# Softmax on the 16 scores a row owns, not on all 128, in the merged attention stage of a two-layer gated transformer

## The reference

```
Q = (layernorm(x) @ Wq.T + bq).reshape(bs, sl, 16, 32)
K = (ctx @ Wk.T + bk).reshape(bs, sl, 16, 32)
V = (ctx @ Wv.T + bv).reshape(bs, sl, 16, 32)
score  = einsum('bshd,bsgd->bshg', Q, K)
weight = softmax(score, axis=-1)            # over the 16 heads g of the same token
attn   = einsum('bshg,bsgd->bshd', weight, V).reshape(bs, sl, 512)
x = x + tanh(g_xattn[1]) * (attn @ Wo.T + bo)
```

## Time and profile before

| | us |
|---|---|
| median of 3 runs | 2135.85 (2131.82 to 2138.77) |
| profiled execution | 2135.37, its span 2133.6 |
| PE busy | 1943.9 (91%) |
| POOL busy | 1085.6 (51%) |
| DVE busy | 993.3 (47%) |
| ACT busy | 832.2 (39%) |
| mean granted TensorE clock | 0.952 of 2.4 GHz |

### The profile page before, as it was taken

The page is one execution under the profiler, slowest core; times in us unless marked ns, Lnnn a source line. Parts: engine busy times, 40 slices in busy tenths (PEclk is TensorE's granted clock), DMA queues, the critical chain, the costliest instruction groups (busy, mean ns, idle before and its releaser), DMA issues. The chain is left out here.

```text
span 2133.6 us, 29710 instructions
## 1 busy us (share of the span) xinstructions
PE 1943.9 (91%) x10300; PEld 1621.4 (76%) x10300; DVE 993.3 (47%) x1565; ACT 832.2 (39%) x1588; POOL 1085.6 (51%) x815
## 2 busy tenths in 40 slices
PE   6999999999999999969999899996499976899998
PEld 5888788878888789847777799995377754678886
DVE  3547654765475556553341233335366343673111
ACT  3327333633354333531112122223277766443332
POOL 5765476548754774442138737514344322844332
PEclk9999999999999999979999899998699977899999
DMA  4231333033322322352327655325678454431000
GB/s 148 95 109 51 114 104 128 30 108 110 109 70 74 124 99 80 120 184 84 126 82 239 215 160 171 115 65 172 171 193 215 125 139 158 159 99 49 20 20 20
DMA packets 172237, 248.12 MB, mean 116 GB/s; under 512 B 44944, under 2 KB 69520, under 8 KB 172112
## 3 DMA queue, kind: packets, MB, share of 16 engines
q1 hardware_dynamic: 157024, 202.09, 30.0%
q0 software_dynamic: 9472, 34.09, 5.0%
q10 hardware_dynamic: 5616, 10.23, 1.2%
HBM read 179.77 MB, written 66.58 MB: 115 GB/s over the span
## 5 line engine op out<-in xcount | busy, mean ns | idle before, releaser
L255 POOL TENSOR_TENSOR a_w_hl<-a_w_raw,a_w_hl 128x2048 fp32r<-128x2048 f32 x63 | 290.7, 4614 | 151.5 <-ACT a_w_hl L320 151.5
L436 PE MATMUL a_proj<-a_c_hl,a_w_hl 128*128 128x512 f32 x768 | 185.1, 401 | 21.0 <-DVE a_w_hl L556 19.8
L436 PEld LDWEIGHTS a_proj<-a_c_hl,a_w_hl 128*128 128x128 f32 x768 | 147.8, 194 | 53.1 <-issue 19.8
L510 PE MATMUL a_proj<-a_w_hl,a_a_hl 128*128 128x512 f32 x768 | 179.5, 392 | 3.9 <-DVE a_a_hl L612 3.9
L320 ACT ACTIVATE a_w_hl<-a_w_raw 128x2048 fp32r<-128x2048 f32 x64 | 122.4, 1912 | 151.7 <-PE a_proj L436 106.7
L436 PE MATMUL a_proj<-a_w_hl,a_c_hl 128*128 128x512 f32 x768 | 181.3, 392 | 0.0
L339 ACT ACTIVATE a_sq<-a_proj,a_vecs 128x512 f32<-128x512 f32 x128 | 88.0, 690 | 232.7 <-PE a_proj L436 160.4
L436 PE MATMUL a_proj<-a_a_hl,a_w_hl 128*128 128x512 f32 x768 | 176.4, 390 | 0.0
L510 PEld LDWEIGHTS a_proj<-a_w_hl,a_a_hl 128*128 128x128 f32 x768 | 142.7, 188 | 34.3 <-POOL a_w_hl L255 5.5
L436 PEld LDWEIGHTS a_proj<-a_a_hl,a_w_hl 128*128 128x128 f32 x768 | 143.6, 188 | 29.7
L279 POOL TENSOR_TENSOR a_ssum<-a_ssum,a_sq 128x512 f32<-128x512 f32 x112 | 145.3, 1297 | 40.1 <-ACT a_sq L339 35.5
(11 more groups left out here) (251 smaller groups left out, 3628.2 us busy)
## 6 DMA issues: line engine op xcount, KB each, us to landing
a_w_raw<-in_a_ki_w SPq DMA_DIRECT2D x16, 1024.0 KB, 5.1
a_w_raw<-in_a_vi_w SPq DMA_DIRECT2D x16, 1024.0 KB, 4.9
a_w_raw<-in_a_q_w SPq DMA_DIRECT2D x16, 1024.0 KB, 4.9
a_w_raw<-in_a_o_w SPq DMA_DIRECT2D x16, 1024.0 KB, 5.3
spare<-in_b_gate_up POOLq DMA_DIRECT2D x32, 352.0 KB, 3.8
l_sorted_rows<-b_zeros SPq DMA_DIRECT2D x39, 256.0 KB, 3.2
spare<-l_sorted_rows SPq DMA_DIRECT2D x39, 256.0 KB, 3.2
l_expert_out<-spare ACTq DMA_DIRECT2D x39, 256.0 KB, 3.5
```

What stands on the lines that cost most here:

```text
L255: pool.tensor_tensor(w_hl[:, s, 1], w_raw[:, s], f32(w_hl[:, s, 0]), ALU.subtract)\
L436: mm = pe.matmul(proj[:, j, :], left, right, start=(k == 0 and n == 0), stop=(k == KC - 1 and n == 2))
L510: mm = pe.matmul(proj[:, j, :], a_hl[:, ap, k, j * P:(j + 1) * P], w_hl[:, i % 2, wp, k], start=(n == 0 and m == 0), stop=(n == 4 * G - 1 ...
```

## The change

In the loop, DVE now multiplies a unit's scores by a 0/1 mask and sums over the 8 tokens of a tile, which leaves each row's own 16 scores (`own_scores`). The maximum, the subtraction, the sum, the reciprocal and the product then run on DVE for a whole pair at once, on 128 x 128 elements (`subtract_max`, `normalise`); ACT takes one exponent per pair, and POOL spreads the result over the 128-wide tile behind the mask (`expand`). `turn` now stands two pairs behind, `weigh` three. The order of items changes too: the prologue holds k, v, h, q of block 0 and k of block 1, the loop then h and v alternately, q, and the next block's k. `move_queries` moves to w = 7, `load_q` to w = 6, the tiles' statistics to w = 4 to 7, the splitting of the context to w = 4 and 5. The low parts of Wq and of context block 1 move from POOL to DVE in the prologue. At each barrier POOL clears the semaphores of the stage before the one that ends, and does so ahead of the barrier.

```diff
-    BIG = 1e30
     RING = 6
-    LAG = 2
+    TURN_LAG, LAG = 2, 3
     IN_QK = NQ * 16
 
-    ITEMS = [(kind, b, j) for kind, b in (("k", 0), ("v", 0), ("h", 0), ("q", 0), ("h", 1), ("q", 1)) for j in range(4)]
+    def four(kind, b):
+        return [(kind, b, j) for j in range(4)]
+
+    ITEMS = four("k", 0) + four("v", 0) + four("h", 0) + four("q", 0) + four("k", 1)
     FIRST = len(ITEMS)
     for n in range(1, NBLK):
-        ITEMS += [("k", n, j) for j in range(4)]
+        ITEMS += [(kind, n, j) for j in range(4) for kind in "hv"] + four("q", n)
         if n + 1 < NBLK:
-            ITEMS += [("v", n, 0), ("h", n + 1, 0), ("v", n, 1), ("h", n + 1, 1), ("h", n + 1, 2), ("h", n + 1, 3),
-                      ("v", n, 2), ("v", n, 3)]
-            ITEMS += [("q", n + 1, j) for j in range(4)]
-        else:
-            ITEMS += [("v", n, j) for j in range(4)]
+            ITEMS += four("k", n + 1)
     NI = len(ITEMS)
     AT = {item: i for i, item in enumerate(ITEMS)}
-    ROUND = {kb: n for n, kb in enumerate((k, b) for k, b, j in ITEMS if k != "h" and j == 0)}
+    ROUND = {item: sum(k != "h" and j == item[2] for k, b, j in ITEMS[:i]) for i, item in enumerate(ITEMS)}
...
+        masked_sc = sb("masked_sc", [P, UN, P])
+        own_sc = sb("own_sc", [P, 3, 2, UN, H])
+        mx = sb("mx", [P, 2, 2 * UN])
+        den = sb("den", [P, 2, 2 * UN])
+        rden = sb("rden", [P, 2, 2 * UN])
...
-        for p in range(12, NP * NBLK):
-            PIECES += [(p, "act")] + ([(p, "dve")] if p >= 20 else [])
+        for p in range(2 * NP, NP * NBLK):
+            PIECES += [(p, "act"), (p, "dve")] if p in (2 * NP + 4, 2 * NP + 5) else [(p, "act")] * 2
...
+                load_ctx(1, j)
+            load_k(0)
             for j in range(TPB):
                 store_x2(0, j)
-            load_k(0)
...
+            store("k", 1, 0)
+            store("k", 1, 1)
             for j in range(TPB):
                 load_x(2, j)
-            for j in range(2):
-                store("q", 1, j)
...
+                    elif w == 5:
+                        load_v(n)
+                        store("q", n, 0)
+                        store("q", n, 1)
+                    elif w == 6:
                         store("q", n, 2)
                         store("q", n, 3)
-                    if w == 1:
...
-            def normalise(u):
-                r = u % RING
-                pool.wait_ge(e_rec, u + 1)
-                pool.tensor_tensor(probs[:, r], probs[:, r], rden[:, r].unsqueeze(2).to_broadcast([P, UN, P]), ALU.mult)\
-                    .then_inc(p_ready, 1)
+            def expand(u):
+                p = u // 2
+                pool.wait_ge(e_done, p + 1)
+                if u >= RING:
+                    pool.wait_ge(av_ready, (u - RING) // 2 + 1)
+                pool.tensor_tensor(probs[:, u % RING].rearrange("p y (g t) -> p y g t", t=TOK),
+                                   own_sc[:, p % 3, u % 2].unsqueeze(3).to_broadcast([P, UN, H, TOK]),
+                                   mask[:].unsqueeze(1).to_broadcast([P, UN, H, TOK]), ALU.mult).then_inc(p_ready, 1)
...
-                n = TPB * (b + 2) + w
-                tile = b + 2 < NBLK and w < TPB
+                n = TPB * (b + 2) + w - 4
+                tile = b + 2 < NBLK and 4 <= w < 4 + TPB
+                if p:
+                    expand(2 * p - 2)
+                    expand(2 * p - 1)
+                low = b + 2 < NBLK and w in (4, 5)
+                if low:
+                    c_low(b + 2, 2 * w - 8)
                 if tile:
                     power(n)
-                normalise(2 * p)
-                normalise(2 * p + 1)
-                if b + 2 < NBLK and w >= NP - KC:
-                    c_low(b + 2, w - NP + KC)
+                if low:
+                    c_low(b + 2, 2 * w - 7)
                 if tile and n + 2 < TPB * NBLK:
                     gather(n + 2)
+            expand(2 * NP * NBLK - 2)
+            expand(2 * NP * NBLK - 1)
...
-            def exponents(u):
-                r = u % RING
-                act.wait_ge(s_max, u + 1)
-                for y in range(UN):
-                    e = act.activation(probs[:, r, y, :], probs[:, r, y, :], ACT.Exp, bias=mx[:, r, y:y + 1],
-                                       accum_out=den[:, r, y:y + 1])
-                e.then_inc(e_ready, 1)
+            def exponents(p):
+                act.wait_ge(s_sub, p + 1)
+                act.activation(rows_of(p), rows_of(p), ACT.Exp).then_inc(e_ready, 1)
...
-                take("q", 1, j)
-                if j == 2:
+                take("k", 1, j)
+                if j == 1:
                     move_queries(0)
             for p in range(NP * NBLK + LAG + 1):
                 b, w = p // NP, p % NP
                 if p < NP * NBLK:
-                    exponents(2 * p)
-                    exponents(2 * p + 1)
                     item_part(2 * p)
-                if p >= 4 and p % 2 == 0:
-                    copy_heads(p // 2 - 2)
-                if 1 <= p <= NP * NBLK:
-                    copy_turned(2 * p - 2)
-                    copy_turned(2 * p - 1)
+                if TURN_LAG <= p < NP * NBLK + TURN_LAG:
+                    copy_turned(2 * (p - TURN_LAG))
+                    copy_turned(2 * (p - TURN_LAG) + 1)
+                if p < NP * NBLK:
+                    exponents(p)
+                if p >= 5 and p % 2 == 1:
+                    copy_heads((p - 5) // 2)
                 if p < NP * NBLK:
                     item_part(2 * p + 1)
-                    if b + 2 < NBLK and w >= NP - KC:
-                        c_high_part(b + 2, w - NP + KC)
-                    if b + 1 < NBLK and w == 3:
+                    if b + 2 < NBLK and w in (4, 5):
+                        c_high_part(b + 2, 2 * w - 8)
+                        c_high_part(b + 2, 2 * w - 7)
+                    if b + 1 < NBLK and w == 7:
...
-                if 1 <= p <= NP * NBLK:
-                    turn(2 * p - 2)
-                    turn(2 * p - 1)
+                if TURN_LAG <= p < NP * NBLK + TURN_LAG:
+                    turn(2 * (p - TURN_LAG))
+                    turn(2 * (p - TURN_LAG) + 1)
...
-            def mask_scores(u):
-                r = u % RING
-                dve.wait_ge(s_ready, u // 2 + 1)
-                if u >= RING:
-                    dve.wait_ge(av_ready, (u - RING) // 2 + 1)
-                dve.tensor_tensor(probs[:, r], sc_ps[:, u % 2],
-                                  mask[:].rearrange("p h t -> p (h t)").unsqueeze(1).to_broadcast([P, UN, P]), ALU.add)\
+            def own_scores(u):
+
+                p = u // 2
+                dve.wait_ge(s_ready, p + 1)
+                if u:
+                    dve.wait_ge(s_gathered, u)
+                dve.tensor_tensor(masked_sc[:], sc_ps[:, u % 2],
+                                  mask[:].rearrange("p h t -> p (h t)").unsqueeze(1).to_broadcast([P, UN, P]), ALU.mult)\
                     .then_inc(s_masked, 1)
+                if p >= 3:
+                    dve.wait_ge(p_ready, 2 * (p - 3) + 2)
                 dve.wait_ge(s_masked, u + 1)
-                dve.tensor_reduce(mx[:, r], probs[:, r], AX.X, ALU.max, negate=True).then_inc(s_max, 1)
-
-            def reciprocal(u):
-                dve.wait_ge(e_ready, u + 1)
-                dve.reciprocal(rden[:, u % RING], den[:, u % RING]).then_inc(e_rec, 1)
+                dve.tensor_reduce(own_sc[:, p % 3, u % 2], masked_sc[:].rearrange("p y (g t) -> p y g t", t=TOK),
+                                  AX.X, ALU.add).then_inc(s_gathered, 1)
+
+            def subtract_max(p):
+                dve.wait_ge(s_gathered, 2 * p + 2)
+                dve.tensor_reduce(mx[:, p % 2], rows_of(p), AX.X, ALU.max).then_inc(s_max, 1)
+                dve.wait_ge(s_max, p + 1)
+                dve.tensor_tensor(rows_of(p), rows_of(p), mx[:, p % 2].unsqueeze(2).to_broadcast([P, 2 * UN, H]),
+                                  ALU.subtract).then_inc(s_sub, 1)
+
+            def normalise(p):
+                dve.wait_ge(e_ready, p + 1)
+                dve.tensor_reduce(den[:, p % 2], rows_of(p), AX.X, ALU.add).then_inc(e_sum, 1)
+                dve.wait_ge(e_sum, p + 1)
+                dve.reciprocal(rden[:, p % 2], den[:, p % 2]).then_inc(e_rec, 1)
+                dve.wait_ge(e_rec, p + 1)
+                dve.tensor_tensor(rows_of(p), rows_of(p), rden[:, p % 2].unsqueeze(2).to_broadcast([P, 2 * UN, H]),
+                                  ALU.mult).then_inc(e_done, 1)
...
+            w_low("q", 0)
             tile_stats(1)
+            w_low("q", 1)
             tile_normalise(0)
+            tile_stats(2)
+            w_low("q", 2)
+            tile_normalise(1)
             dve.wait_ge(const_in, 32)
             take_v(0, 0)
-            tile_stats(2)
-            tile_normalise(1)
             take_v(0, 1)
             tile_stats(3)
+            w_low("q", 3)
             tile_normalise(2)
```

(38 more changed lines are left out.)

79 lines of the change are left out of this document (30 added, 49 removed).

## The result

The changed kernel takes 2107.9 us (median of 4 runs, 2103.4 to 2110.1), the kernel before 2134.0 beside it: a ratio of 0.987, interval 0.985 to 0.990. The profiled execution took 2103.4 us, with a span of 2101.6. Forecast were 2078, a range of 2057 to 2105, and a gain of 57.5 us; 26.1 came by the medians and 32.0 in the profiled execution, so the time lies above the range.

What follows compares the result with a forecast made beforehand. It took waits among engines to bound prologue and bare pairs (a ring through the softmax), and PE the first pairs. Prologue 33.7, loop 16 and two barriers at 3.9 sum to 57.5: 2135.4 to 2078 us, range 2057 to 2105.

Steps and rivals of the forecast that it cites:

- The prologue: Merged stage's start to first scores: 33.7 us less, including 5.7 from the barrier; between 24 and 38 in other cases.
- Barriers: Starts of three stages: clearings no longer delay first work, 5.7 us within the prologue and 3.9 at each other stage.
- The cover for the moved clearings is POOL's idle time at a stage's end: Ahead of the barriers: POOL's idle time hides the clearings; without it they cost their own 4 to 6 us again.
- the chain is not what binds: Rival, chance 0.05: DMA holds bare pairs and prologue; only the barriers' 13.5 and little more return, 2122 us or more.
- Low parts, 1 us at two places: Loop at w = 5: the next block's keys wait for POOL's last `c_low`, 1 us at two places.
- `move_queries` at two block ends, 2.5 each: Loop at w = 7: the move stands on ACT behind the last item's take, 2.5 us standstill twice, 5 in all.
- The 4 us for odd waits: Loop up to pair 22: 4 us added for odd waits like those the first 20 pairs have today.
- Bare pairs: Pairs without items: steps of 5.1 us, nine steps 46, with two holds 57, against 63 at today's 7.02.
- The hold by the queries in pair 23: Before pair 24: `load_q(3)` stands on SP behind piece loads, so the queries are moved late, a hold of 4.3 us.
- The hold by the 12 loads: Last block, w = 3 and 4: SP's head stores and 12 next-stage loads delay ACT's pieces, 6.5 us within the bare pairs.
- The chain shrinks less: Rival, chance 0.25: expansions at 1.63, DVE waiting for POOL in every pair, later landings; 20 to 30 us, about 2102.
- the prologue's weak end: Prologue gain of only 24 us, if tiles' data come as late as before and the queries' round trip is longer.

Runs made afterwards that it cites:

- clears_behind: The changed kernel with each stage's semaphores cleared behind its barrier, as in the kernel before: 2104.6 us, 0.985 of the kernel before.
- clears_inside: The changed kernel with the previous stage's clearings as POOL's last instructions inside the running stage's block: 2094.5 us, 0.979 of the kernel before.
- highs_at_4: The changed kernel with all four high parts made by ACT at w = 4 and both w = 5 low parts ahead of POOL's power: 2097.9 us, 0.983.
- next_early: The changed kernel with the last stage's 12 loads issued at pairs 23 (four) and 25 (eight) instead of 28: 2102.8 us, 0.985 of the kernel before.

## Why the prediction was wrong

- **The sign and the mechanism** of the prologue and of the bare pairs were right. The size was wrong: of the 57.5 us, 25.5 didn't come in the profiled execution and 31.4 by the medians, half of the 25.5 at the barriers.
- **The prologue** gave 32.3 of 33.7, in part by luck. The first h item stands 33.9 behind the stage's start (I had 32.4), the queries take 11.2 at the full clock (13.1), and from their last item to the first scores it is 15.7 (13.8; the terms of that way, two landings of 4.9 and 2 for the issues, make 11.8, and I added 10.8). Over the ten profiles of this prologue the gain is 27 to 34 against the 98.2 and 97.9 of the two with the old one.
- **Barriers, the largest miss (13.4).** The step "The cover for the moved clearings is POOL's idle time at a stage's end" failed. I took its price in the same breath ("their own 4 to 6 us again") and gave it next to no weight: only a part of the rival "the chain is not what binds" held it, at 0.03. The gains behind the barriers came (4.1, inside the prologue, 3.8), but 3.7, 5.4 and 4.3 were lost ahead of them. `clears_behind` and `clears_inside` show it. The idle time that I read off lies before the block's exit; the clearings stand behind it, where the engines have met already. That the exit is a meeting of its own is read from these rows, not from a view that shows it.
- **Low parts, 1 us at two places: measured 7.8 each (13.7 too little).** I added up POOL's work and didn't follow the high parts on ACT, which stand behind the exponents and the last take, and the exponents behind DVE. `highs_at_4` brings both pairs to 9.5. By the sum of POOL's work alone the term of 1 was nearly right, 0.8.
- **`move_queries` at two block ends, 2.5 each:** the wait was 2.1, but the half clock behind it cost 1.6 more. The 4 us for odd waits didn't come. Together the 22 pairs took 184.5 instead of 171.
- **Bare pairs:** 50.6 for nine steps instead of 57. The steps are 4.5, not 5.1, and DVE's load, 4.1 of them where I had 4.7, sets them. The hold by the queries in pair 23 was 7, not 4.3; no run was made for it.
- **Tail, 12.1 unchanged: 18.2.** The hold by the 12 loads, which I put at 6.5 into the bare pairs, came behind the last scores. ACT's wait of 8.54 there is 7.5 from the piece's issue to its use, behind 3 MB of other loads, and only 1.1 of SP's issuing. `next_early` takes 4.9 of it back.
- **Operations.** Spreading: 1.08 for 1.2. The short DVE operations on 128 elements: 0.28 to 0.29 for the 0.23 of the mask's row (the reciprocal, on 8, 0.20); the estimate from the Trainium skill (VectorE: DVE Perf Modes, "The TRN2 errata", which states it for adds of two tensors), 0.29, was the better one, and the row I set against it was a poor neighbour. Contention: the subtraction mostly took 0.60 (0.29 to 0.67), when POOL spread the pair before; the product, with POOL waiting for it, 0.29. So it costs 0.3 a pair, where I had 0.8. This agrees with the Trainium skill (GPSIMD Engine Reference, "8. Key points") on DVE instructions with two SBUF inputs. A larger price was nowhere in the sum: 1.2 for a tile's normalising beside a low part, four times.
- **The rivals.** "The chain shrinks less" stood at 2102, and its own terms make more: 0.9 to 1.5 in 22 pairs are 20 to 33, and the prologue's weak end is another 9.7, which gives 2108 to 2121. The measured 2107.9 is near it, but not for its reasons: the expansion was cheaper than forecast and the prologue not at its weak end. The queue on ACT stood in none of the cases, and the exit of the block in none as a cause.

## What to carry to other kernels

Before work is called covered by an engine's idle time, find the instruction between them: idle time before a block's exit covers nothing behind it. When a step is moved, follow each of its producers through its own queue, one engine further than the engine that PE waits for. Transfers that only need to be there at the end of a stage don't belong in front of small ones that an engine waits for.
